# Cross-attention and expert network on one core: scores of two head groups in one burst, engine orders for two bursts per batch

## The reference

```python
q = (query @ Wq + bq).reshape(b, sq, N_HEAD, KEY_DIM)      # 16 heads of 64
k = (key @ Wk + bk).reshape(b, key.shape[1], N_HEAD, KEY_DIM)
v = (value @ Wv + bv).reshape(b, value.shape[1], N_HEAD, VALUE_DIM)
scores = jnp.einsum('bqhd,bkhd->bhqk', q, k) / TEMP
attn = jax.nn.softmax(scores, axis=-1)
out = jnp.einsum('bhqk,bkhd->bqhd', attn, v).reshape(b, sq, N_HEAD * VALUE_DIM)
out = out @ Wo + bo + residual        # then a layer norm with gamma, beta, and x + ...
```

## Time and profile before

| | before |
|---|---|
| median of 3 runs | 1743.85 us (1738.86 to 1746.9) |
| profiled execution, first to last instruction | 1733.9 us |
| busy over the span: PE / PEld / DVE / ACT / POOL | 86% / 73% / 75% / 59% / 25% |
| score matmuls (L1360) | 1024 instructions, 149.7 us busy |
| first and last score burst start | 725.04 and 1377.42 us |

### The profile page before, as it was taken

How to read it: one execution, slowest core, us unless ns; L and a number is a source line. 1 busy time by engine, 2 the same in 40 slices (tenths; PEclk the granted TensorE clock), 3 DMA queues, 4 the chain that set the end, 5 groups by cost and what they waited for, 6 DMA issues and landing times. The chain is left out here.

```text
span 1733.9 us, 35773 instructions
## 1 busy us (share of the span) xinstructions
PE 1496.1 (86%) x11323; PEld 1266.4 (73%) x11323; DVE 1298.2 (75%) x2223; ACT 1020.1 (59%) x2527; POOL 433.8 (25%) x638
## 2 busy tenths in 40 slices
PE   3899999699961078799999999999999838999897
PEld 2455555388840078789999999989999728988897
DVE  6988888677788987466777776677776578888786
ACT  2566666455587453565566666666665406877675
POOL 3211111000000002112222222222222236666666
PEclk9999999899996589899999999999999769999998
DMA  5410101000051023401111110110000046311110
GB/s 189 139 33 29 33 27 34 14 0 1 0 167 63 0 74 114 142 13 29 32 32 32 38 35 30 30 30 30 30 27 26 13 162 255 133 41 46 43 47 19
DMA packets 66241, 96.75 MB, mean 56 GB/s; under 512 B 10214, under 2 KB 57327, under 8 KB 63346
## 3 DMA queue, kind: packets, MB, share of 16 engines
q1 hardware_dynamic: 60546, 83.16, 14.5%
q0 software_dynamic: 5616, 12.60, 2.3%
HBM read 76.57 MB, written 21.90 MB: 57 GB/s over the span
## 5 line engine op out<-in xcount | busy, mean ns | idle before, releaser
L1663 ACT ACTIVATE c_w_raw<-c_ps_score,c_shift 128x128 f32<-128x128 f32 x512 | 182.0, 374 | 66.2 <-DVE c_shift L1524 66.0
L1360 PE MATMUL c_ps_score<-c_kT,c_qT 64*128 64x128 f32 x1024 | 149.7, 287 | 0.0
L2051 PE MATMUL d_ps_hT<-d_zT,d_w_tile 128*128 128x128 f32 x1248 | 147.5, 277 | 2.5 <-DVE d_zT L2156 2.5
L805 PE MATMUL b_ps<-b_down_high,b_inner 128*128 128x256 f32 x384 | 71.7, 290 | 87.9 <-DVE b_inner L1087 87.9
L2051 PEld LDWEIGHTS d_ps_hT<-d_zT,d_w_tile 128*128 128x128 f32 x1248 | 144.4, 194 | 3.2 <-DVE d_zT L2156 3.2
L362 PE MATMUL a_ps_score<-a_keys,a_qT 128*128 128x512 f32 x256 | 137.0, 617 | 3.8 <-ACT a_qT L552 2.2
L1360 PEld LDWEIGHTS c_ps_score<-c_kT,c_qT 64*128 64x128 f32 x1024 | 125.0, 189 | 19.9 <-issue 9.8
L1685 ACT ACTIVATE c_qT<-c_ps_proj,c_bq 128x256 f32<-128x256 f32 x128 | 55.0, 497 | 141.4 <-PE c_ps_proj L1390 137.7
L1334 POOL TENSOR_TENSOR c_var_o<-c_mv_o,c_eps 128x1 f32<-128x1 f32 x32 | 6.8, 211 | 517.8 <-DVE c_mv_o L1582 517.8
L2064 PE MATMUL d_ps_y<-d_w_parts,d_hT 128*128 128x256 f32 x936 | 127.4, 295 | 1.8 <-DVE d_res L2183 1.8
L2222 ACT ACTIVATE d_h<-d_ps_hT,d_b1T 128x128 f32<-128x128 f32 x312 | 88.7, 366 | 64.6 <-PE d_ps_hT L2051 64.6
(11 more groups left out here) (260 smaller groups left out, 3782.1 us busy)
## 6 DMA issues: line engine op xcount, KB each, us to landing
d_w<-w_in SPq DMA_DIRECT2D x16, 1024.0 KB, 8.0
b_x_space<-w_in SPq DMA_DIRECT2D x16, 512.0 KB, 3.6
a_x<-x_in SPq DMA_DIRECT2D x4, 1024.0 KB, 7.6
a_keys<-ctx_blocks_in SPq DMA_DIRECT2D x128, 32.0 KB, 2.1
a_v_raw<-ctx_in SPq DMA_DIRECT2D x4, 1024.0 KB, 8.8
x_scratch<-a_x SPq DMA_DIRECT2D x32, 128.0 KB, 1.7
b_x_space<-x_scratch SPq DMA_DIRECT2D x32, 128.0 KB, 2.4
x_scratch<-b_x_space SPq DMA_DIRECT2D x32, 128.0 KB, 2.0
```

Source lines behind the costliest of these rows:

```text
L805: last = pe.matmul(ps[:, t, 0:D], inner[:, s, a, f, t * P:(t + 1) * P], down_parts[b][:, f, :], start=(j == 0), stop=(j == NF * len(PARTS) ...
L1360: last = pe.matmul(ps_score[:, n % 2, j, :], qT[rows, s, blk, tok], kT[rows, s, blk, tok], start=True, stop=True)
L1663: last = act.activation(prob[:, n, j, :], ps_score[:, n % 2, j, :], ACT.Exp, scale=float(KD) ** -0.5, bias=shift[:, n, j:j + 1], accum_out ...
L2051: last = pe.matmul(ps_hT[:, f, :], w1_tile[:, half, k, n * P:(n + 1) * P], zT[:, s, k, :], start=(k == 0), stop=(k == ND - 1))
```

## The change

`scores` now takes a column group instead of a unit. One call issues the eight matmuls of two units and alternates the row half from one matmul to the next: even ones go into bank 0 from the upper 64 rows, odd ones into bank 1 from the lower 64. It waits until the exponentials of both units of the burst before are done. `maxima` waits for the burst. The step of each engine is written anew for two bursts a step. In the new order PE does all four transposes of two units in one go, `output` stands between the two halves of `values`, `split_attn` and `copy_attn` of the first half move to the start of the next step, and `turn_x` stands after the first half of `keys`. All operations, sizes and buffers are otherwise as they were.

```diff
-                def scores(b, u, n):
-                    g, r = divmod(n, 2)
+                def scores(b, u, g):
...
-                    if inside(b, 1, NB) or n >= 2:
-                        pe.wait_ge(exp_done, NU * b + n - 1)
-                    for j in range(HB):
-                        blk = HB * g + j
-                        last = pe.matmul(ps_score[:, n % 2, j, :], qT[rows, s, blk, tok], kT[rows, s, blk, tok],
+                    if inside(b, 1, NB) or g == 1:
+                        pe.wait_ge(exp_done, NU * b + 2 * g)
+                    for j, r in product(range(HB), range(2)):
+                        blk, rows = HB * g + j, slice(r * KD, (r + 1) * KD)
+                        last = pe.matmul(ps_score[:, r, j, :], qT[rows, s, blk, tok], kT[rows, s, blk, tok],
                                          start=True, stop=True)
                     last.then_inc(scores_done, 1)
...
-                    dve.wait_ge(scores_done, m)
+                    dve.wait_ge(scores_done, 2 * b + n // 2 + 1)
```

More of the change, by code:

```diff
@@ L1473, in step @@
                 def step(b, u, i):
[L1474 to L1504, removed]
@@ new lines, in step @@
+                    here, back = inside(b, 0, NB - 1), inside(b, 1, NB)
+                    if here:
+                        scores(b, u, 0)
+                    queries(b, u, 0)
+                    if inside(b, 4, NB + 3):
+                        turn_z(b, u)
+                    if back:
+                        transposes(b - 1, 2)
+                        transposes(b - 1, 3)
+                    queries(b, u, 1)
+                    if inside(b, 4, NB + 3):
+                        logits_of(b - 4)
@@ new lines, in step @@
+                    keys(b, u, 0, i)
+                    if inside(b, FIRST, NB - 5):
+                        turn_x(b, u)
+                    if back:
+                        weighted(b - 1, (u - 1) % 4, 1)
+                    if here:
+                        scores(b, u, 1)
+                    keys(b, u, 1, i)
+                    if here:
+                        transposes(b, 0)
+                        transposes(b, 1)
+                    values(b, u, 0)
+                    if back:
+                        output(b, u)
@@ L1619, in step @@
                         normalise(b + 4, u, None if i is None else i + 2)
[L1620 to L1649, removed]
@@ new lines, in step @@
+                    if here:
+                        divide(b, 0)
+                        divide(b, 1)
+                    if isinstance(b, int) and (b, 0) in split_at:
+                        rest_of_weights(split_at[b, 0])
+                    if inside(b, FIRST, NB - 5):
+                        split_x(b, u)
+                    if inside(b, 3, NB + 2):
+                        normalise_routed(b - 3, (u + 1) % 4, turn[3])
+                    if back:
+                        split_attn(b - 1, (u + 1) % 2, 1)
@@ new lines, in step @@
+                    if isinstance(b, int) and (b, 1) in split_at:
+                        rest_of_weights(split_at[b, 1])
+                    if u % 2 == 1 and inside(b, -3, NB - 5):
+                        split_context(b, u)
+                    if here:
+                        maxima(b, 2)
+                        maxima(b, 3)
+                        divide(b, 2)
+                    if inside(b, *projects):
+                        copy_values(b, u, 0)
+                    if here:
+                        divide(b, 3)
@@ L1651, in step @@
+                    if back:
+                        add_residual(b - 1, (u + 1) % 2)
+                    if inside(b, *projects):
+                        copy_values(b, u, 1)
+                    if isinstance(b, int) and (b, 3) in split_at:
+                        rest_of_weights(split_at[b, 3])
+                    if back:
                         output_statistics(b - 1, (u + 1) % 2)
```

79 lines of the change are left out of this document (48 added, 31 removed).

## The result

| | before | after |
|---|---|---|
| median of 4 runs beside each other | 1741.36 us | 1662.26 us (1661.1 to 1667.86) |
| profiled execution | 1733.9 us | 1660.6 us |
| ratio, 95% interval | | 0.955 (0.952 to 0.958) |

The change makes the kernel 4.5% faster. I had said 1686 us, between 1666 and 1731: right in sign and in the mechanism, but the time lies 3.7 us under the range.

A forecast was written before the change was run, and what follows sets the result against it. PE was taken to set the 20.82 us step; with paired bursts and a DVE/ACT ring, 18.9. Thirty steps x 1.92 = 57.6 us, none for the last two: profiled 1733.9 to 1676.3, median 1743.85 to 1686, range 1666 to 1731.

The forecast's parts named there:

- the low end: Whole kernel: 1666 us, if borders shrink to half, steps take 18.4 us and the two last steps give 6 us together.
- PE's own step: PE's work per step in the attention loop, without waits: from 20.82 to 18.64 us if row halves pair, else 20.40.
- steps 30 and 31: Last two steps with scores, no projections left: from no change to 6 us less each; none was taken.
- Row halves pair: In score bursts, upper-row and lower-row instructions run side by side: 16 take 1.09 us, saving 2.18 us a step.
- The count of loads in flight: Evidence for pairing: at 849.53 us `weighted` has two weight loads in flight, where the score burst has one.
- The doubt about equal columns per microsecond: `weighted` and score bursts load nearly the same columns per microsecond, which a single load path without pairing would give as well.
- the term for the borders: Time PE loses at the two borders of a score burst: 0.21 us a burst, with two bursts a step instead of four.
- The ring: DVE and ACT operations waiting on each other round a loop step: 18.61 us, 18.95 with `split_context`, 18.27 without; 18.9 taken.
- Profiled execution to median: Whole kernel: the median of runs lies 10 us above the profiled span, so 1676.3 us profiled becomes 1686.
- No pairs: Rival, score bursts: loads go one by one, burst 1.97 us, PE's step 20.40, total 1730 us (1722 to 1738); chance 0.16.
- Longer ring: Rival, loop: pairs hold but DVE and ACT bound steps at 19.9 to 20.3 us, total 1700 to 1720; chance 0.08.
- Each change drains: Rival, score bursts: each row-half change costs a border, burst 3.5 us, PE's step 23.5, total 1829 us; chance 0.06.

## Why the prediction was right or wrong

- **Why outside the range.** The time saved at the median is 79.1 us (1741.36 less 1662.26). I gave 57.6, and 78 at the low end. Of the 3.7 us below the range 1.1 are this; the other 2.5 are that the kernel before measured 1741.36 beside the new one and not the 1743.85 from which I counted. The terms that made 57.6 too small are PE's own step and steps 30 and 31, below; the mechanism held.
- **Row halves pair: right.** Burst 1.09 for 1.09; without pairs 1.98 for 1.97. The row I leaned on, `weighted` at 0.064 us an instruction, was the right neighbour. The count of loads in flight, two for one, was weaker than I took it, as loads 0.19 long that start 0.11 apart are two at some instants without any pairing. The doubt about equal columns per microsecond was unfounded: 16 x 128 columns are loaded in the 0.97 us that 8 x 128 took. The Trainium skill (TensorE: Matmul & The Clock Gate, Part 3) has loads overlap where row groups differ; the burst of one row half alone, 1.98 us, and the alternating one, 1.09, agree with that part.
- **PE's own step, 18.64: wrong by 0.40.** The step that failed is the term for the borders, 0.21 a burst, with "all other PE groups keep their number". They kept their number and not their time. I had measured only the half of a border that lies in the burst; the other half lies in the neighbour, as in the last matmul of `keys` ahead of a border. And the wide spacing went with the old order. I had taken the border too small (0.105 for 0.14). The lower end of the range made it smaller still, which was the wrong direction: fewer borders are worth more if a border is dear.
- **The ring, 18.61, and 18.9 taken: right in kind.** The loop ran at 18.66 in the mean, but that takes in its first four steps, which PE sets (18.24 to 18.32). From b 14 on the mean is 18.76, with steps of about 18.4 and 19.1 in turn where I had 18.27 and 18.95. So the ring was some 0.15 longer than its sum, and my 18.80 came near it with a wrong part, PE's 18.64 in place of the shorter steps: that is luck. PE waits where I said; against the 18.24 of a step without waits the loop loses 0.42 a step, where I had allowed some 0.3. ACT waits long for the shift ahead of the first exponentials too (2.87 us at 906.57), which I had not said.
- **Steps 30 and 31 "at none": wrong by 9.9 us.** I gave "from no change to 6 us less each" and took the end of the range for no reason but doubt. Step 30 alone gave 7.2, above my bound, of which some 3.7 to 4.2 are read as clock: the row that showed a clock of 0.75 there was taken as a fact about the chain and not as a cost that a denser order can give back. The rest are rounds, which the term had at nothing too.
- **First four steps, 2.5 us, and steps 28 and 29, 1.5 us more than given:** PE sets the last two (18.01 for 20.65), so they got the whole of the missed 0.4 and no ring. Of the first four, step 0 alone gave 3.1 (16.81 to 13.71).
- **Profiled execution to median: 10 us added, 1.7 found.** The span of before lay 10 us under the median of its runs and that of after 1.7 under. The miss of 23.7 us at the median is 15.7 in the span and 8.0 here. In every run listed the time is 1.7 to 1.8 us above the span of the same run; the other 8 are that the profiled execution of before was a short one. Such an offset is chance and belongs in the width of the range, not in its middle.
- **Rivals.** *No pairs*, forecast 1730: the kernel with both units from the upper rows measured 1710 against 1662, so the price of the pairing was about right (44 forecast, 48 measured) and the rest, some 20 us, is the error that both sums share. In part this is luck, as 5 of the 48 are step 30, which I had given no price. *Longer ring*: not at the size that I gave it; no stretch of the loop had steps over 19.2 us. *Each change drains*: a burst would have been 3.5 us; it is 1.09.

## What to carry to other kernels

Where two groups of small matmuls use different row halves of the array, issue them in one burst and alternate; with four instructions of one half in a row a burst of 16 loses about 0.1 us, and with eight in a row more than half of the gain. Count a border between tile forms on both sides of it, 0.14 us in the one place measured here, and price an order of PE by its borders, not by its matmuls alone. Where a stretch runs at a lower granted clock behind waits of PE, an order that closes the waits can earn the clock as well (step 30 did, step 31 did not), so give it a term and a range of its own. After the bound engine has been relieved, look at which copies it then waits for: here two moved copies and an early read were worth another 10 us.

## What the runs showed of the hardware that I had not expected

- Equal matmuls of 128x256 stand 0.113 or 0.118 us apart, mostly for a whole group: 2.72 or 2.83 us for the 24 of `output`. What decides it is open.
- Eight instructions of one row half followed by eight of the other take 1.64 us, less than the 1.98 of one half alone: by slots and by starts, PE overlaps across the change by about three instructions. In the alternating burst the first two instructions, one of each half, are recorded 0.37 us long and the others 0.27. In this run the first is 0.37 long and then the sixth to start, at 842.61, though the first of the lower half is the ninth in the program. As I read it, a lower one started ahead of three upper ones; the records don't name the half.
- Some of DVE's operations are longer while POOL works. Three DVE groups of the kernel before, the same three after, and one of them with both units from the upper rows, 800 to 1240 us (busy us, mean ns):

```profile
L1596 DVE TENSOR_TENSOR c_x<-c_proj,c_x_late 128x256 f32<-128x256 f32 x21 | 16.9, 803 | 1.6
L1591 DVE TENSOR_TENSOR c_proj<-c_proj,c_gamma 128x256 f32<-128x256 f32 x21 | 16.1, 765 | 0.7
...
L1588 DVE TENSOR_SCALAR c_proj<-c_proj,c_mv_o,c_rstd_o 128x256 f32<-128x256 f32 x21 | 10.9, 521 | 0.0
```

```profile
L1584 DVE TENSOR_SCALAR c_proj<-c_proj,c_mv_o,c_rstd_o 128x256 f32<-128x256 f32 x23 | 20.7, 902 | 0.0
...
L1587 DVE TENSOR_TENSOR c_proj<-c_proj,c_gamma 128x256 f32<-128x256 f32 x23 | 10.2, 444 | 0.8
...
L1592 DVE TENSOR_TENSOR c_x<-c_proj,c_x_late 128x256 f32<-128x256 f32 x23 | 9.8, 425 | 1.7
```

```profile
L1584 DVE TENSOR_SCALAR c_proj<-c_proj,c_mv_o,c_rstd_o 128x256 f32<-128x256 f32 x22 | 8.9, 406 | 0.0
```

The same addition is 803 ns beside POOL's residual operations and 425 ns without them; the scaling ahead of it, which after runs beside them, went from 521 to 902. With both units from the upper rows the orders and operations are those of the kernel after, but POOL's residual operations are nearly over when the scaling starts (one of them runs from 861.49 to 862.22, the scaling from 862.26), and it is 406. It isn't so for every operation: the products of probabilities (L1528) take 692 ns with and without POOL at work. That POOL is the cause is argued from this; no run moves POOL alone. The sum per step is 2.09 us before and 1.77 after, a gain of 0.3 on DVE that was in no term of mine.

- ACT's exponentials grew from 375 to 399 ns (reads of the sums from 212 to 238). It goes with the new orders and not with how dense the bursts are: with the short bursts in the old orders they are 374 and 212, with the long bursts of one row half in the new orders 399 and 238. Their starts stay 0.35 us apart (906.57, 906.92), so the ring pays nothing for it. Why is open.
